# Gated cross-attention and mixture-of-experts layer: the values' product and output projection moved one step later, odd probabilities turned by VectorE

## What is computed

```
h   = layernorm(x)
q   = h @ Wq.T      (32 heads of 128)          q = rmsnorm(q) * q_norm_w
k,v = ctx @ Wk.T, ctx @ Wv.T (8 heads of 128)  k = rmsnorm(k) * k_norm_w
p   = softmax(q k^T / sqrt(128) + mask)        (64 x 64 per sequence and head)
x   = x + tanh(g_xattn) * (p v) @ Wo.T
h2  = layernorm(x)
x   = x + tanh(g_ffn) * (top-2-of-16 experts(h2) + shared expert(h2))
```

## Time and profile before

| | us |
|---|---|
| runs, median of 3 (lowest to highest) | 1366.54 (1366.28 to 1366.75) |
| profiled execution, its own time | 1367.91 |
| its span, first to last instruction | 1366.2 |
| TensorE busy / share of the span | 1351.8 / 99% |
| VectorE busy / share | 1041.6 / 76% |
| ScalarE busy / share | 505.4 / 37% |
| GpSimd busy / share | 359.9 / 26% |
| mean granted clock of TensorE | 0.999 |

### The profile page before, as it was taken

The page is one execution under the profiler, slowest core; times in us unless marked ns, Lnnn a source line. Parts: engine busy times, 40 slices in busy tenths (PEclk is TensorE's granted clock), DMA queues, the critical chain, the costliest instruction groups (busy, mean ns, idle before and its releaser), DMA issues.

```text
span 1366.2 us, 24589 instructions
## 1 busy us (share of the span) xinstructions
PE 1351.8 (99%) x8473; PEld 1092.8 (80%) x8474; DVE 1041.6 (76%) x2190; ACT 505.4 (37%) x1085; POOL 359.9 (26%) x375
## 2 busy tenths in 40 slices
PE   8999999999999999999999999999999999999998
PEld 7888877888888888888888888888887888777777
DVE  6676668898888888898988888888687655334459
ACT  4233244343434444344334343434344321222242
POOL 1122232212121221212121212122112100467746
PEclk9999999999999999999999999999999999999999
DMA  6766631222122221222121222212222344555548
GB/s 208 248 190 204 187 112 40 59 56 72 50 57 66 62 59 47 76 53 59 50 78 48 59 63 66 55 51 59 55 78 85 132 171 161 193 185 162 168 158 297
DMA packets 178209, 146.13 MB, mean 107 GB/s; under 512 B 77376, under 2 KB 139328, under 8 KB 177856
## 3 DMA queue, kind: packets, MB, share of 16 engines
q1 hardware_dynamic: 170592, 120.17, 29.4%
q0 software_dynamic: 7520, 24.65, 5.4%
HBM read 97.06 MB, written 47.71 MB: 106 GB/s over the span
## 4 chain that ended last, share of the span: by engine, by line
PE 80%; DVE 3%; issue 1%; DMA 0%; ACT 0%; POOL 0%; DVEq 0%; ACTq 0%
PE ps L677 20%; PE ps L679 19%; PE ps L678 19%; PE ps L1071 6%; PE ps L761 5%; PE ps L808 4%; PE ps L1087 3%; PE ps L1066 2%; PE ps L793 1%; DVE acc L2086 1%; DVE acc L2093 1%; PE ps L984 1%; PE ps L816 0%; PE ps L1118 0%; PE ps L769 0%
## 5 line engine op out<-in xcount | busy, mean ns | idle before, releaser
L574 POOL CAST vth<-vt 128x256 fp32r<-128x256 f32 x64 | 25.4, 397 | 538.6 <-PE ps L808 536.6
L1268 ACT CAST ah<-ps 128x256 fp32r<-128x256 f32 x256 | 83.1, 381 | 208.4 <-PE ps L679 202.0
L677 PE MATMUL ps<-hT,w0h 128*128 128x512 f32 x384 | 152.2, 396 | 1.2 <-DVE w0l L1542 1.2
L679 PE MATMUL ps<-hT,w0h 128*128 128x512 f32 x384 | 149.8, 390 | 0.0
L678 PE MATMUL ps<-hT,w0l 128*128 128x512 f32 x384 | 149.6, 390 | 0.0
L568 POOL TENSOR_TENSOR qr<-qv,mhalf 128x8 f32<-128x8 f32 x64 | 105.1, 1642 | 139.2 <-DVE qv L1672 113.5
L1228 ACT ACTIVATE qs<-ps,wqk 128x512 f32<-128x512 f32 x128 | 88.2, 689 | 125.8 <-PE ps L679 125.8
L1623 DVE TENSOR_TENSOR acc<-ps,acc 128x512 f32<-128x512 f32 x128 | 88.0, 687 | 50.5 <-PE ps L679 50.3
L677 PE MATMUL ps<-w0l,ah 128*128 128x512 f32 x256 | 105.9, 414 | 0.0
L1241 ACT ACTIVATE pb<-pb 128x256 f32<-128x256 f32 x128 | 48.3, 419 | 154.4 <-DVE pb L1692 154.4
L677 PE MATMUL ps<-w1l,ah 128*128 128x512 f32 x256 | 105.1, 411 | 0.0
(11 more groups left out here) (255 smaller groups left out, 3172.8 us busy)
## 6 DMA issues: line engine op xcount, KB each, us to landing
wraw<-in_w_att SPq DMA_DIRECT2D x64, 256.0 KB, 2.7
vbuf<-vo SPq DMA_DIRECT2D x16, 512.0 KB, 3.3
kbuf<-ko SPq DMA_DIRECT2D x16, 512.0 KB, 5.3
kt<-kbuf SPq DMA_DIRECT2D x128, 64.0 KB, 2.2
vt<-vbuf SPq DMA_DIRECT2D x64, 128.0 KB, 2.2
wgu<-in_w_gu SPq DMA_DIRECT2D x4, 2048.0 KB, 7.9
y<-ybuf SPq DMA_DIRECT2D x16, 512.0 KB, 6.9
pbuf<-pbT SPq DMA_DIRECT2D x26, 256.0 KB, 2.0
```

Source lines behind the costliest of these rows:

```text
L677: pe.matmul(dst, l_hi, r_lo, start=first, stop=False)
L679: return pe.matmul(dst, l_hi, r_hi, start=False, stop=last)
L1268: act.copy(ah[:, bp, :, b2, :], pv_view(bp, b2)).then_inc(a_hi, 1)
```

## The change

Every engine's program of the steps is rewritten for a pipeline that is one step longer, and the loops over steps are written out:

- TensorE's step i does `probs_v(i-2)` instead of `probs_v(i-1)`, the projection of the second half of i-3 and the first half of i-2. The small product `add_quarters` now stands between the two projections. The first small product is for step 4 instead of 3; step 3 has `q_sums`.
- Probabilities of all steps from 2 to 56, odd and even, are turned by VectorE and go through memory. `turn_probs(i)` is the first thing in VectorE's step i. No transpose by TensorE is left in those steps. The odd step's half is read back once the even step's half is split (there is one tile `pt_raw`), and its cast stands ahead of the exponentials in ScalarE's queue.
- SyncE's step i: store of the turned tile of step i, in odd steps the keys, then weights' slice, reads of `pt_raw`, values (for even steps the slice comes last).
- GpSimd splits the values of step j-2 ahead of the root of step j.
- Step 56 (`catch_up`) does what is one step behind: two values' products and two pairs of projections; steps 57 to 63 go as before. The opening has one values' product and one pair of projections less.
- VectorE's remainder of a weights' slice of an odd step moves into the next step's softmax, beside the root.

The diff, cut to its core:

```diff
-BY_DMA = (4, STEPS - NC)
-TURNED = (3, STEPS - NC + 1)
+BY_DMA = (2, STEPS - NC + 1)
+TURNED = (4, STEPS - NC + 1)
...
 # SyncE
+            def probs_out(i):
+                sp.wait_ge(p_turned, i - BY_DMA[0] + 1)
+                if i > BY_DMA[0]:
+                    sp.wait_ge(p_back, 64 * (i - BY_DMA[0]))
+                sp.dma_start(pbuf, pbT[:].rearrange("p c m i -> p c (m i)")).then_inc(p_out, 16)
+
+            def probs_back(i):
+                sp.wait_ge(p_out, 16 * (i - BY_DMA[0] + 1))
+                sp.wait_ge(pT_evac, 2 * i)
+                for c in range(4):
+                    sp.dma_start(pt_raw[32 * c:32 * c + 32].rearrange("p q m i -> p q (m i)"),
+                                 p_ld[c]).then_inc(p_back, 16)
+
+            for i in range(STEPS - NC + 1):
+                if by_dma(i):
+                    probs_out(i)
+                if i % 2:
+                    sp.wait_ge(s_done, i + 1)
+                    load_k(i // 2 + 1)
+                if i == 0:
+                    load_v(1)
+                if i % 2 or not by_dma(i):
+                    load_slice(i)
+                if by_dma(i):
+                    probs_back(i)
+                    load_v(i)
+                if i % 2 == 0 and by_dma(i):
+                    load_slice(i)
...
 # TensorE
+            def step(i):
+
+                next_query(i)
+                probs_v(i - 2, i % 2)
+                scores((i + 1) // 2, (i + 1) % 2)
+                pe.wait_ge(acc_done, 2 * (i - 2) + 1)
+                project_out(1, att(i - 3), (0, 1, 2, 3))
+                if i + 1 == TURNED[0]:
+                    pe.wait_ge(const_dve, 6)
+                add_quarters(i + 1)
+                if i % NC == 2:
+                    pe.wait_ge(w_lo, i + 6)
+                projected_0(i - 2, att(i - 2))
+
+            def catch_up(i):
+
+                next_query(i)
+                probs_v(i - 2, 0)
+                scores((i + 1) // 2, (i + 1) % 2)
+                q_sums(i + 1)
+                pe.wait_ge(acc_done, 2 * (i - 2) + 1)
+                project_out(1, att(i - 3), (0, 1, 2, 3))
+                projected_0(i - 2, att(i - 2))
+                probs_v(i - 1, 1)
+                pe.wait_ge(acc_done, 2 * (i - 1) + 1)
+                project_out(1, att(i - 2), (0, 1, 2, 3))
+                projected_0(i - 1, att(i - 1))
...
 # ScalarE
+            def probs_hi(i, odd, bank=2):
+                if by_dma(i):
+                    act.wait_ge(p_back, 64 * (i - BY_DMA[0] + 1))
+                    act.wait_ge(pv_done, 2 * i + 2 - 2 * odd)
+                    act.copy(raw_view(0, odd), pt_raw[:]).then_inc(pT_hi, 2)
...
+            def act_step(i):
+
+                queries(i)
+                a_hi_tile(i - 2, 0)
+                if i % 2:
+                    probs_hi(i - 1, 0)
+                a_hi_tile(i - 2, 1)
+                split_slice(i, att(i + NC), i % NC)
+                if i % 2:
+                    probs_hi(i, 1)
+                exps(i + 1)
...
 # VectorE
+            def dve_step(i):
+
+                odd = i % 2
+                late = i % 2 == 1 and 3 < i < STEPS - NC - 1
+                turn_probs(i)
+                turn_squares(i + 1, 0)
+                sum_squares(i + 1, 0)
+                if odd:
+                    slice_lo(i - 1, att(i + NC), i % NC - 1)
+                turn_squares(i + 1, 1)
+                sum_squares(i + 1, 1)
+                split_sums(i + 1)
+                a_rest(i - 2, 0)
+
+                def while_root():
+                    if odd:
+                        probs_lo(i - 1, 0)
+                    elif i > 4:
+                        slice_lo(i - 1, att(i - 1 + NC), (i - 1) % NC)
+                    add_out(2 * i - 3, 1, (2 * i - 5) % NT)
+                    a_rest(i - 2, 1)
+
+                def while_exp():
+                    add_out(2 * i - 2, 0, (2 * i - 4) % NT)
+
+                softmax(i + 1, while_root, while_exp, turn_before=i - BY_DMA[0] + 1)
+                if odd:
+                    probs_lo(i, 1)
+                    if not late:
+                        slice_lo(i, att(i + NC), i % NC)
```

More of the change, by code:

```diff
@@ L305, in rows_by_pe, with by_dma, pT_before, att @@
             return isinstance(n, int) and (n < 2 or n == NT - 1)
[L307 to L317, removed]
+        def by_dma(i):
+            return BY_DMA[0] <= i < BY_DMA[1]
+        def pT_before(i):
+            return i if i < BY_DMA[0] else i - (BY_DMA[1] - BY_DMA[0])
+        def att(r):
+            return W[r // NC % 2]
+        def raw_view(x_, odd):
+            return pt[x_][:, :, odd * P:odd * P + P].rearrange("p m (q i) -> p q m i", q=4)
         def turned(j):
@@ L430, in next_loads @@
                 sp.dma_start(wraw[:], w_att[i + NC]).then_inc(wr_in, 16)
-                for n in x_tiles:
+            def probs_out(i):
[24 more added lines that the diff above has]
+                    load_slice(i)
+            load_v(STEPS - NC + 1)
+            for t in range(1, NC - 1):
+                i = STEPS - NC + t
+                if t % 2:
+                    sp.wait_ge(s_done, i + 1)
+                    load_k(i // 2 + 1)
+                load_slice(i)
+                if t == 1:
+                    sp.wait_ge(pT_evac, 2 * BY_DMA[1])
+                for n in {1: (0, 1), 2: ()}.get(t, (2 * t - 4, 2 * t - 3)):
                     if n >= 2:
@@ L434, in next_loads @@
                     sp.dma_start(xt3[n % 2][:], x[n]).then_inc(x3_in[n % 2], 16)
[L435 to L458, removed]
+                load_v(i + 1)
             def store_h2(n):
@@ L590, in _ @@
             split_v(1)
-            split_v(2)
-            with pool.Fori(3, STEPS - 2) as j:
+            inverse_root(3)
+            with pool.Fori(4, STEPS - NC + 2) as j:
+                split_v(j - 2)
+                inverse_root(j)
+            split_v(STEPS - NC)
+            split_v(STEPS - NC + 1)
+            for j in range(STEPS - NC + 2, STEPS - 2):
                 inverse_root(j)
@@ L841, in outputs @@
                 project_out(0, w_o, (0, 1, 2, 3))
[L843 to L848, removed]
+            def outputs(r, w_before, w_o, o_ready=None):
+                pe.wait_ge(acc_done, 2 * r + 1)
+                project_out(1, w_before, (0, 1, 2, 3))
+                if o_ready is not None:
+                    pe.wait_ge(w_lo, o_ready)
+                pe.wait_ge(pT_evac, 2 * r + 4)
+                projected_0(r, w_o)
@@ new lines, in next_query @@
+            def next_query(i):
+                if i % NC == NC - 1:
+                    pe.wait_ge(w_lo, i + 5)
+                for h in range(2):
+                    pe.wait_ge(q_sq, 2 * i + 1 + h)
+                    q_head(h, (i + 1) % 2, (i + 1) % NC // 2, att(i + 1)).then_inc(q_done, 1)
+            def step(i):
[10 more added lines that the diff above has]
+                projected_0(i - 2, att(i - 2))
@@ L913, in opening @@
                 scores(1, 1)
[L914 to L938, removed]
+                q_sums(3)
+            opening()
+            for i in range(3, STEPS - NC):
+                step(i)
+            catch_up(STEPS - NC)
+            for i in range(STEPS - NC + 1, STEPS - 1):
+                last_step(i, o_ready=STEPS if i == STEPS - NC + 1 else None, last=(i == STEPS - 2))
             r = STEPS - 2
@@ L1273, in split_slice, with queries, act_catch_up, act_last @@
                          w[0][:, sl * 512:(sl + 1) * 512], wraw[:]).then_inc(w_hi, 1)
-            def act_step(d, odd, w, sl):
-                i = 2 * d + odd
+            def queries(i):
+                act.wait_ge(s_done, i + 1)
+                for h in range(2):
+                    q_out(h, i + 1)
+                    squares(h, i + 1)
+            def act_step(i):
[5 more added lines that the diff above has]
+                split_slice(i, att(i + NC), i % NC)
+                if i % 2:
+                    probs_hi(i, 1)
+                exps(i + 1)
+            def act_catch_up(i):
+                queries(i)
+                a_hi_tile(i - 2, 0)
+                a_hi_tile(i - 2, 1)
+                split_slice(i, att(i + NC), i % NC)
+                exps(i + 1)
+                a_hi_tile(i - 1, 0)
+                a_hi_tile(i - 1, 1)
+                probs_hi(i, 0)
+            def act_last(i):
                 act.wait_ge(s_done, i + 1)
```

194 lines of the change are left out of this document (72 added, 122 removed).

## The result

| | before | after |
|---|---|---|
| runs, median (lowest to highest) | 1366.41 (1365.63 to 1366.75), 4 runs | 1551.40 (1541.62 to 1555.25), 4 runs |
| profiled execution | 1367.91 | 1541.62 |
| its span | 1366.2 | 1539.8 |
| TensorE busy / share | 1351.8 / 99% | 1398.0 / 91% |
| mean granted clock | 0.999 | 0.948 |

The ratio is 1.134, with a 95% interval of 1.130 to 1.139: 13% slower, where the prediction had 1496 (9.5%) and a range up to 1530. The profiled execution is the fastest of the changed kernel's; the others have a clock of 0.943 to 0.947 and lie 8 to 14 us above it.

A forecast was written before the change was run, and what follows sets the result against it. TensorE, busy 99% of the span, was taken as the bound. From 1366.5 us, -13.9 + 99.9 + 2 + 32.4 + 7.8 + 0.5 + 1.3 = +130 gave 1496, range 1445 to 1530.

The forecast's parts named there:

- transposes off TensorE: TensorE's attention steps: 27 odd steps lose 0.48 us each, steps 2 and 56 lose 0.45 each; -13.9 us, the whole gain.
- wait for keys, with step 3: Odd steps' scores wait 3.7 us for key loads queued behind SyncE's store; 27 times, +99.9, plus 2 for step 3.
- clock: TensorE's clock falls to 1.2 GHz around the odd steps' gaps; 1.2 us each, 27 times, +32.4 us.
- even steps' values' product: In even steps TensorE waits 0.3 us for the remainder of the odd step's probabilities; 26 times, +7.8 us.
- catch-up step: Seam where the last projection waits for the whole softmax and two subtractions; about +1.3 us, bounds 0 to 3.
- the working to 10.15 of the step: Odd step: transpose ends 5.7, store 5.84, first key load 6.46, last 7.95, landing 10.15; scores start 10.2 instead of 6.43.
- three falls in four: Share of odd-step gaps taken to lower TensorE's clock, giving 1.2 us per odd step, between bounds 0 and 1.6.
- the 1.6 of the earlier trace: Cost in us of the one clock fall in the old kernel's opening: nine product intervals in 3.65 instead of 2.07.
- The rival with the clock holding: Same odd-step wait for keys, but TensorE keeps 2.4 GHz through the gaps: 1464 us, chance 0.22.
- the half microsecond of step 3's sums: Seam: step 3 keeps the old way of the sums, 0.57 us of products instead of 0.11; +0.5 us.
- slower loads: Rival: store and loads share engines, key loads take their upper bound, 1.5 us more 27 times: 1536 us, chance 0.09.
- keys in time: Rival: the softmax chain is 3.7 us shorter, so odd steps' keys land by 6.43: 1362 us, chance 0.06.

The follow-up runs named there:

- the best kernel: Changed kernel with keys ahead of the store, small product mid-projection, exponentials ahead of the reloaded half's cast, and step 2's slice load first: 1359.41 us, ratio 0.9951.
- third experiment: Changed kernel with the small product back after two of the first projection's four heads, keys still behind the store: 1483.57 us, ratio 1.0865.
- fourth experiment: Changed kernel with key loads ahead of the store, and VectorE's remainder subtractions ahead of the softmax instead of beside the root: 1365.87 us, ratio 0.9995.
- first: Changed kernel with the four key loads queued ahead of the store of turned probabilities in SyncE's odd steps: 1375.08 us, ratio 1.0068.
- fifth: Changed kernel with key loads ahead of the store, and the small product back after two of the first projection's four heads: 1363.81 us, ratio 0.9978.
- sixth experiment: Changed kernel with key loads ahead of the store, and ScalarE's exponentials ahead of the reloaded odd half's cast: 1372.80 us, ratio 1.0047.
- the seventh: Changed kernel with key loads ahead of the store, small product mid-projection, and exponentials ahead of the reloaded half's cast: 1362.67 us, ratio 0.9970.

## Why the prediction was wrong

The mechanism held, in the place named and in both its parts; what failed are sizes, the clock's above all, then the wait's and that of one small term. Term by term, the profiled executions differing by 173.7:

| term | predicted | measured |
|---|---|---|
| transposes off TensorE | -13.9 | -13.9 as reckoned; the odd step without a gap is 13.22, 0.49 shorter |
| wait for keys, with step 3 | +101.9 | +115.5, 27 waits |
| clock | +32.4 | +45 to 53 |
| even steps' values' product | +7.8 | +11.3 |
| catch-up step | +1.3 | +1.2 |

**Transposes.** Right. Nothing replaced them in TensorE's list.

**The keys.** Right that the odd step's scores wait for them, 27 times. The step that was mis-sized is the working to 10.15 of the step; the scores start at 10.55. The quotient ends at 5.21 instead of 4.97, since the root on GpSimd takes 2.01 instead of 1.64 and VectorE waits 0.26 for it. The first load follows the store by 0.36, where I had 0.62 from a spacing behind another DMA: 6.35 instead of 6.46. The four loads take 2.21 (1.92 in the earlier trace rows), and the landing has a median of 2.4 instead of 2.2. A gap is then 4.1 on average instead of 3.7, which lies inside my bounds of 2.8 and 5.2. Step 3 waits 8.3, where I had 3.7 + 2.

**The clock.** This is the step that failed: "three falls in four", at 1.2 per step. It fell in every odd step, and one fall costs more than the 1.6 of the earlier trace rows. Behind the gap the 32 narrow products of the scores stretch from 1.15 to between 1.76 and 1.98 us, and the next products start 0.43 to 0.59 apart, where 0.23 is usual. That by itself is no dearer per microsecond than the wide products of the earlier trace rows; the slow stretch is longer. It was 3.65 us there; here products start 0.43 apart until 2.9 to 6.3 us behind the start of the scores, 4.5 on average. That the fall may come while TensorE still waits is true of some gaps (in step 25 the windows view has 0.51 from 602 to 604, two us in which TensorE only waits), but it saves little there: the clock is back at 1.00 only from 609 on, 4.7 behind the scores' start. What sets the length of the slow stretch stays open. From the scores of the odd step to those of the even one are 15.78 on average, against 13.82 in the kernel with the filled gap, which gives 2.0 per gap and 53 for 27; the pairs of that kernel (31.43 against 33.21) give 46, its profiled execution 45, its median 54. The filled gap itself is 0.17 longer by these intervals, 4.5 over the 26 pairs, which accounts for the difference between 51 (26 times 1.96) and 46. The rival with the clock holding, to which I gave 0.22, is refuted by each of these rows. Its argument, that 26 us of full work stand between gaps, held behind none of the 27.

The Trainium skill (TensorE: Matmul & The Clock Gate, HAM oscillation) describes a kernel in which the DMA wait of each tile drops the clock for the next one, in every tile. The trace agrees: 27 gaps, a fall in each. With a fall in each and the 1.6 of the earlier trace rows the sum would have been 1506, nearer than what I took, and still short by what the longer slow stretch and the longer gap add.

**The even steps.** Predicted 0.3 for the remainder of the odd probabilities, measured 0.43 per pair. I had the chain from the reload through the exponentials. The runs show that only single long steps come from it (the longest wait 1.4 goes to 0.4 without it); the usual part is the chain from the small product with the root's 0.37 in it, since either mending of that chain takes it away.

**Sum.** The measured terms with the half microsecond of step 3's sums are -13.9 + 115.5 + 53 + 11.3 + 0.5 + 1.2 = 168 against 173.7. The 6 us between them lie in distances that are longer than the idle time shown: the odd step's scores come 4.21 later where 4.12 of waiting is listed, the even step's in the kernel with the filled gap 0.60 where 0.45 is listed. What remains against the runs is that the median lies 9.8 above the profiled execution. The clock differs between these runs (0.943 to 0.948); which gaps make the difference stays open, since only one of them has a trace. My range ended at 1530. The wait and the clock at their measured sizes bring the forecast there by themselves (1496 + 13.6 + 20.6 = 1530), so the even steps' 3.5 more, the 6 without a term and the 9.8 all fall outside. I had given the clock and the wait an upper bound each but had not laid the cases together: slower loads plus a fall in every gap, from my own rows, is 1536 + 11 = 1547.

**What was not predicted:** that the loss could be mended by order alone. The prediction priced the change as it stands, and its rival "keys in time" asked for a shorter softmax. Keys in time through another place in the queue give 1375, and with three more changes of order 1359.

Of the 13.9 us of the transposes the best kernel keeps 6.9 by the medians, 8.6 by the profiled executions. Its pair is 26.50, 0.44 shorter than before, 11.4 us over the 26 pairs, where 12.5 were to be had. Outside them, where 1.4 were to be had, it loses 2.7 by the profiled executions: 1.2 is the catch-up step's wait, the rest lies in the opening, where the waits of 2.1 and 1.5 stand.

## What to carry to other kernels

An in-order DMA queue needs the same care as an engine: before a load that another engine will need soon, look for what its predecessor waits on, and put the load with the late need ahead of any entry whose wait ends late. Price a gap of TensorE twice, as the wait and as the slow stretch behind it, and count the slow stretch behind every gap. Its length varied here from 2.9 to 6.3 us, so the single one of an earlier trace is a poor measure of it. When a result is moved later, ask what new operation runs beside the short one on the critical chain.

## What the runs showed that I had not expected

- **Useless work that pays.** 55 bf16 products on constants in each gap made the kernel 54 us faster than leaving the gap empty. In the third experiment a gap of 2.48 already lowered the clock, with 0.43 between starts behind it, as did 25 others of 2.49 to 8.4; the one of 2.47 in step 53 didn't (scores 1.15, 0.23 between starts behind them).
- **A subtraction beside the root slows the root.** GpSimd's operation on 128x8 numbers takes 1.64 us before the change, 1.64 with the subtraction moved away, and 2.01 in each of the 42 steps of the changed kernel that the view above has, where VectorE subtracts one tile in SBUF from another beside it:

```profile
577.17 0.68 DVE L1746 TENSOR_TENSOR ptl<-pt_raw,pth 128x512 fp32r<-128x512 f32 x1
```

```profile
577.34 2.01 POOL L579 TENSOR_TENSOR qr<-qv,mhalf 128x8 f32<-128x8 f32 x1 [8.41 <-DVE qv L1712]
```

The subtraction started 0.17 before the root; the next one on VectorE starts at 577.77, 0.43 after the root did, and the root is 0.37 longer. Before, `add_out` stood there, which reads PSUM. GpSimd's own subtraction (`vtl`, L587) has a median of 0.73 in both kernels, and at most 1.06 before and 1.28 after. The 1.28 stands beside a subtraction on VectorE (`slice_lo` at 567.66):

```profile
567.65 1.28 POOL L587 TENSOR_TENSOR vtl<-vt,vth 128x256 fp32r<-128x256 f32 x1
```

The Trainium skill (SBUF — State Buffer, SBUF: two separate sides) says that a VectorE operation with two inputs in SBUF and a GpSimd operation that reads SBUF exclude each other for the whole instruction. The trace agrees in kind: the 0.37 lost is close to the 0.43 for which the two overlap. That only the subtraction's place matters is shown, by the fourth experiment; that it is the reading of SBUF is the skill's account, and no run tells it from another.

- **Reloads have a tail.** The reads of the probabilities land in a median of 1.9 us, and the slowest one takes 3.2 to 3.8 in four kernels (first, fourth, fifth and sixth experiment). One late reload in ScalarE's queue ahead of the exponentials makes its whole step 0.6 to 1 us longer, and a schedule reckoned from medians leaves that out. My expectations of the fourth to seventh experiments were reckoned so and came out 6 to 14 us too low; how much of that is this tail isn't shown, and not all of it is, since in the seventh nearly every step is 13.23 and 6 us are missing all the same, outside the pairs.
